# Row maxima of half the score units added on VectorE instead of by a matmul, with all orders drawn anew

## The reference, cut to what matters

```python
h = layernorm(x) * g1 + b1
x = attention(h, h) + x             # 16 heads of 64, 1024 keys: "self"
h = layernorm(x) * g2 + b2
x = attention(h, context) + x       # 16 heads of 64, 154 keys: "cross"
h = layernorm(x) * g3 + b3
p = h @ w1 + b; a, gate = halves of p   # 2 x 1024 columns
x = (a * gelu(gate)) @ w2 + b2 + x
# attention: softmax(q k^T / 8) v for each head, then @ wo + bo
```

## Time and profile before

| | |
|---|---|
| median of 3 runs | 1222.76 us (1222.62 to 1223.83) |
| profiled execution | 1222.66 us, span 1220.6 us |
| TensorE busy | 1186.3 us, 97% of the span |
| VectorE | 767.2 us, 63% |
| ScalarE | 642.3 us, 53% |
| GpSimd | 743.0 us, 61% |
| granted TensorE clock, mean | 0.997 |

### The profile page before, as it was taken

One profiled execution on the slowest core, in us unless ns is written; L12 is line 12 of the kernel. 1 busy time (PEld: TensorE's weight loads), 2 busy tenths in 40 slices (PEclk: granted clock), 3 DMA queues, 4 the chain that ended last, 5 costly groups with the idle time before them and its releaser, 6 DMA issues.

```text
span 1220.6 us, 23620 instructions
## 1 busy us (share of the span) xinstructions
PE 1186.3 (97%) x9385; PEld 776.6 (64%) x9385; DVE 767.2 (63%) x1289; ACT 642.3 (53%) x954; POOL 743.0 (61%) x381
## 2 busy tenths in 40 slices
PE   3899999999999999999999999999999999999998
PEld 3655665566566656666655664666666666678887
DVE  4757566575575576675665756458777877674433
ACT  3447554445445446744544454557855586536432
POOL 1196787886876976877877768864556346321000
PEclk9899999999999999999999999999999999999999
DMA  3010000000000000000000000011111110010000
GB/s 111 14 27 10 6 17 16 5 11 23 6 10 23 6 10 23 6 10 14 14 11 12 10 13 6 23 31 50 48 40 32 33 33 14 15 36 18 18 18 18
DMA packets 63539, 25.76 MB, mean 21 GB/s; under 512 B 34551, under 2 KB 61383, under 8 KB 63431
## 3 DMA queue, kind: packets, MB, share of 16 engines
q1 hardware_dynamic: 63375, 24.25, 7.6%
q10 hardware_dynamic: 56, 0.01, 0.0%
HBM read 21.62 MB, written 2.10 MB: 19 GB/s over the span
## 4 chain that ended last, share of the span: by engine, by line
PE 89%; POOL 4%; ACT 2%; DVE 2%; issue 1%; DMA 1%; SPq 0%; DVEq 0%; POOLq 0%; ACTq 0%
PE psum L858 22%; PE psum L844 22%; PE psum L736 15%; PE psum L721 9%; PE psum L881 7%; PE psum L821 6%; POOL acc L1402 4%; PE psum L941 4%; PE psum L869 3%; PE psum L826 2%; PE psum L895 1%; ACT probs L1273 1%; DVE xr L1084 1%; DMA probs<-in_ctx 1%; DVE m_part L1047 1%
## 5 line engine op out<-in xcount | busy, mean ns | idle before, releaser
L1402 POOL TENSOR_TENSOR acc<-acc,probs 128x1024 f32<-128x1024 f32 x192 | 458.7, 2389 | 70.1 <-ACT probs L1273 49.7
L1273 ACT ACTIVATE probs<-psum 128x1024 f32<-128x1024 f32 (+1 forms) x320 | 317.1, 1031 | 275.6 <-PE psum L844 271.1
L1047 DVE TENSOR_REDUCE m_part<-psum 128x2 f32<-128x1024 f32 x256 | 308.9, 1222 | 223.0 <-PE psum L821 223.0
L858 PE MATMUL psum<-probs,val 128*64 128x512 f32 x1024 | 244.9, 603 | 0.0
L1402 POOL TENSOR_TENSOR acc<-probs 128x1024 f32<-128x1024 f32 (+1 forms) x64 | 152.8, 2388 | 142.2 <-ACT probs L1273 120.3
L1084 DVE SCALAR_TENSOR_TENSOR xr<-psum,d_cols,xr 128x256 f32<-128x256 f32 x512 | 207.8, 476 | 35.1 <-PE psum L881 34.6
L858 PEld LDWEIGHTS psum<-probs,val 128*64 128x64 f32 x1024 | 63.3, 136 | 113.7 <-issue 98.8
L844 PE MATMUL psum<-row_max,minus 64*128 64x512 f32 (+1 forms) x640 | 125.9, 389 | 0.0
L844 PE MATMUL psum<-q_hi,k_hi 64*128 64x512 f32 x512 | 101.6, 393 | 0.3 <-DVE m_part L1047 0.3
L844 PE MATMUL psum<-q_lo,k_hi 64*128 64x512 f32 x512 | 100.8, 389 | 0.0
L844 PE MATMUL psum<-q_hi,k_lo 64*128 64x512 f32 x512 | 100.8, 389 | 0.0
(11 more groups left out here) (147 smaller groups left out, 2132.1 us busy)
## 6 DMA issues: line engine op xcount, KB each, us to landing
xr<-in_x SPq DMA_DIRECT2D x8, 256.0 KB, 5.8
wv_raw<-in_L_xattn_sa_wv SPq DMA_DIRECT2D x8, 256.0 KB, 2.9
wqk_raw<-in_L_xattn_sa_wq SPq DMA_DIRECT2D x16, 128.0 KB, 2.5
wqk_raw<-in_L_xattn_sa_wk SPq DMA_DIRECT2D x16, 128.0 KB, 2.3
wo_raw<-in_L_xattn_sa_wo SPq DMA_DIRECT2D x16, 128.0 KB, 2.4
d_cols<-d_rows SPq DMA_DIRECT2D x128, 2.0 KB, 2.1
wqk_raw<-in_L_xattn_ca_wq SPq DMA_DIRECT2D x16, 128.0 KB, 2.6
probs<-in_L_xattn_ff_w SPq DMA_DIRECT2D x8, 256.0 KB, 3.4
```

What stands on the lines that cost most here:

```text
L858: mm = pe.matmul(psum[d, PVB + half, :], values(J)[0:plan.ks, kt, own], probs[buffer_of(J, u)][0:plan.ks, h, :], start=(kt == 0), stop=(kt ...
L1047: dve.tensor_reduce(m_part[:, half, :, t, kh], psum[:, bank0:bank0 + 2, :], AX.X, ALU.max).then_inc(s_x_read, 1)
L1273: act.activation(probs[buffer_of(J, u)][0:plan.ks, :, :], psum[0:plan.ks, bank0:bank0 + 2, :], ACT.Exp, scale=SCALE).then_inc(s_exp, 1)
L1402: pool.tensor_tensor(total, last if kt == 1 else total, now, ALU.add).then_inc(s_acc, 1)
```

## The change

Units 1, 3, 5, ... 15 of each self pair (`TAKEN_BY_VECTOR`) lose the fourth step. VectorE instead adds a block `less_max` (minus the maxima, spread over all 128 partitions) to the scores while it moves them from PSUM to `probs`; this is the new item U, function `take`. ScalarE then takes their exponential in place. The PSUM buffer of such a unit is given back by U. The even units keep the fourth step, now with `one_row` (ones in rows 0 and 64) and the same `less_max` block.

The maxima of a half, now negated in the reduction, go by one DMA into a scratch tensor in DRAM (M), and from there by one DMA to all 128 partitions (N). N waits for M to land and for all users of the old block. The cross pairs keep their way and use the `less_max` blocks as their buffer; their M waits for that. All written orders are new.

```diff
+TAKEN_BY_VECTOR = (1, 3, 5, 7, 9, 11, 13, 15)
+def on_vector(J, u):
+    return J < NSELF and u in TAKEN_BY_VECTOR
+def taken(J, u):
+    return min(J, NSELF) * len(TAKEN_BY_VECTOR) + sum(v < u for v in TAKEN_BY_VECTOR if J < NSELF)
...
-MOVED = before(lambda p: 16 * 2)
+MOVED = before(lambda p: 16 if p.own else 32)
...
 SELF_ORDER = {
+    "sp": "G@-197.68 W@-114.85 M0@-11.44 N0@-10.62 M1@14.11 N1@27.09 O@38.83 T@53.64",
+    "pe": "P12-@-5.74 K0+@-3.73 S0@-3.58 K1+@-2.78 P13-@-1.64 P14-@-1.42 P15-@-0.29 D-@0.24 S1@3.54 Q0+@4.03 S2@4.11 Q1+@6.99 S3@7.94 Y0.0-@8.14 P0@8.41 P1@8.74 S4@10.18 X0+@10.20 S5@10.42 Y0.1-@10.69 S6@11.02 X1+@12.19 P2@12.57 S7@12.72 Y1.0-@12.98 Y1.1-@15.66 X2+@16.27 P3@16.82 P4@17.25 P5@17.65 X3+@19.47 S8@20.20 X4+@21.02 P6@21.03 S9@21.84 S10@22.09 S11@22.49 X5+@23.04 P7@23.63 P8@23.64 X6+@25.24 X7+@28.87 V0++@30.48 X8+@32.24 V1++@33.23 S12@33.68 S13@34.94 S14@36.14 X9+@36.81 P9@38.15 P10@39.08 P11@39.13 X10+@40.69 S15@41.30 X11+@45.63 X12+@47.02 X13+@47.46 X14+@47.67 X15+@50.32",
+    "dve": "K0+@2.17 K1+@2.88 L1-@7.22 U1@7.73 B-@8.41 U3@9.16 Q0+@9.53 Q1+@11.36 Y0.0-@13.06 X0+@13.32 U5@14.63 Y0.1-@14.99 X1+@15.49 U7@16.29 Y1.0-@17.34 Y1.1-@19.07 X2+@22.43 X3+@29.20 X4+@29.36 U9@29.96 U11@30.37 X5+@30.70 X6+@30.75 X7+@32.90 C0+@34.86 X8+@35.42 U13@37.07 X9+@37.17 X10+@40.85 U15@42.12 X11+@42.16 L0@48.43 X12+@50.77 X13+@56.12 X14+@56.78 X15+@57.47 C1+@58.36",
...
 def release_of(item):
     if kind == "S":
-        return "S", U0[J] + a + 1
+        return ("U", taken(J, a) + 1) if on_vector(J, a) else ("S", U0[J] + a + 1)
...
-        top = [sb(f"row_max{b}", [P, SEQ], F32R) for b in range(2)]
-        minus = sb("minus", [P, P], F32R)
+        less_max = [sb(f"less_max{a}", [P, 2, HALF], F32R) for a in range(2)]
+        one_row = sb("one_row", [P, P], F32R)
...
+        max_rows = nc.dram_tensor("less_max_rows", (2, 2, HALF), F32, kind="Internal").ap()
...
             def move_m(J, a):
...
+                if own:
+                    sp.dma_start(max_rows[a].rearrange("h (p t) -> p h t", p=P),
+                                 m_cols[a][:].bitcast(F32).rearrange("p (h t) -> p h t", h=2)).then_inc(s_m[a], 16)
+                    return
...
+            def spread_m(J, a):
+                sp.wait_ge(s_m[a], MOVED[J + 1])
+                if J:
+                    sp.wait_ge(s_s, U0[J - 1] + 8 * (a + 1))
+                    sp.wait_ge(s_taken, taken(J - 1, 8 * (a + 1)))
+                sp.dma_start(less_max[a][:].bitcast(F32), max_rows[a].partition_broadcast(P)).then_inc(s_less_max[a], 16)
...
             def S(J, u):
...
+                last = 2 if on_vector(J, u) else 3
+                for i, (w, x) in enumerate(((k_hi, q_hi), (k_hi, q_lo), (k_lo, q_hi))):
                     for h in range(2):
+                        mm = pe.matmul(psum[0:plan.ks, bank_of(("S", J, u), h), :], w[rows_of(h), ks], x[rows_of(h), qs], start=(i == 0), stop=(i == last))
+                if last == 3:
+                    for h in range(2):
+                        x = less_max[half][rows_of(h), h, :] if plan is SELF else top[J % 2][rows_of(h), qs]
+                        mm = pe.matmul(psum[0:plan.ks, bank_of(("S", J, u), h), :], one_row[rows_of(h), 0:plan.ks], x, start=False, stop=True)
...
+            def take(J, u):
+                half = u // SELF.kt
+                bank0 = bank_of(("S", J, u))
+                back = user_before(J, u)
+                dve.wait_ge(s_less_max[half], 16 * (J + 1))
+                if back:
+                    dve.wait_ge(s_pv, U0[back[0]] + back[1] + 1)
+                    dve.wait_ge(s_acc, added(*back))
...
+                dve.wait_ge(s_s, U0[J] + u + 1)
+                dve.tensor_tensor(probs[buffer_of(J, u)][:], psum[:, bank0:bank0 + 2, :], less_max[half][:].bitcast(F32), ALU.add).then_inc(s_taken, 1)
...
             def S(J, u):
...
+                if on_vector(J, u):
+                    act.wait_ge(s_taken, taken(J, u) + 1)
+                    act.activation(p, p, ACT.Exp, scale=SCALE).then_inc(s_exp, 1)
+                    return
```

More of the change, by code:

```diff
@@ L161 @@
     "sp": "",
[L162 to L165, removed]
+    "pe": "t0.0@13.94 t0.1@15.70 t1.0@28.06 t1.1@35.50",
+    "dve": "n0@-14.00 n1@-10.99 z0@-7.55 z1@-0.19 l0.0@18.73 l0.1@21.95 l1.0@31.17 l1.1@39.39",
+    "act": "s0@-6.00 y0@-0.00 a0.0@15.35 a0.1@17.36 y1@19.46 a1.0@25.62 a1.1@39.37",
+    "pool": "b0@12.93 b1@62.78",
 }
@@ L473, in block_kernel @@
         w2_lo = [w2_lo_both[:, 4 * i:4 * i + 4, :].rearrange("p f c -> p (f c)") for i in range(2)]
+        top = [t[:].rearrange("p h n -> p (h n)") for t in less_max]
+        max_rows = nc.dram_tensor("less_max_rows", (2, 2, HALF), F32, kind="Internal").ap()
         z_early = acc[1][:].rearrange("p h n -> p (h n)").rearrange("p (t d) -> p t d", t=4)
@@ L483, in block_kernel @@
         s_fill = sem("buffers_filled")
-        s_minus_zero = sem("minus_zeroed")
+        s_row_zero = sem("one_row_zeroed")
         s_vec = sem("vectors_loaded")
@@ L523, in block_kernel @@
         s_m = [sem(f"m_moved{a}") for a in range(2)]
+        s_less_max = [sem(f"less_max{a}_ready") for a in range(2)]
+        s_taken = sem("max_taken")
         s_s = sem("s_ready")
@@ L646, in move_m @@
                     sp.wait_ge(s_x_read, X0[J + 1])
-                if J < 2:
-                    sp.wait_ge(s_fill, FILLS)
-                if J >= 2:
-                    sp.wait_ge(s_s, U0[J - 1])
-                n = 4 if own else 8
-                for h in range(2):
-                    row, q0 = h * DH, a * HALF
-                    cols = m_cols[a] if own else c_cols[J % 2]
-                    sp.dma_start(top[J % 2][row:row + 1, q0:q0 + n * P].bitcast(F32).rearrange("o (p t) -> o p t", p=P),
-                                 cols[:, n * h:n * (h + 1)].bitcast(F32)).then_inc(s_m[a], 16)
+                if own:
+                    after(sp, s_less_max[a], 16 * J)
+                else:
+                    sp.wait_ge(s_s, U0[J if J == NSELF else J - 1])
+                    sp.wait_ge(s_taken, taken(J, 0))
+                if own:
+                    sp.dma_start(max_rows[a].rearrange("h (p t) -> p h t", p=P),
+                                 m_cols[a][:].bitcast(F32).rearrange("p (h t) -> p h t", h=2)).then_inc(s_m[a], 16)
+                    return
+                for h in range(2):
+                    sp.dma_start(top[J % 2][h * DH:h * DH + 1, :].bitcast(F32).rearrange("o (p t) -> o p t", p=P),
+                                 c_cols[J % 2][:, 8 * h:8 * (h + 1)].bitcast(F32)).then_inc(s_m[a], 16)
+            def spread_m(J, a):
[4 more added lines that the diff above has]
+                sp.dma_start(less_max[a][:].bitcast(F32), max_rows[a].partition_broadcast(P)).then_inc(s_less_max[a], 16)
             def move_d(J):
@@ L699, in _ @@
                     move_m(J, a)
+                elif kind == "N":
+                    spread_m(J, a)
                 elif kind == "T":
@@ L838, in S @@
                     pe.wait_ge(s_kq_lo, KQ0[J] + plan.khalf + half + 1)
-                    pe.wait_ge(s_m[half if plan is SELF else 0], MOVED[J + 1])
+                    if plan is CROSS:
+                        pe.wait_ge(s_m[0], MOVED[J + 1])
+                if plan is SELF and not on_vector(J, u):
+                    pe.wait_ge(s_less_max[half], 16 * (J + 1))
                 ks = slice(kt * plan.ks, (kt + 1) * plan.ks)
                 qs = slice(half * HALF, (half + 1) * HALF)
-                for i, (w, x) in enumerate(((k_hi, q_hi), (k_hi, q_lo), (k_lo, q_hi), (minus, top[J % 2]))):
+                last = 2 if on_vector(J, u) else 3
+                for i, (w, x) in enumerate(((k_hi, q_hi), (k_hi, q_lo), (k_lo, q_hi))):
                     for h in range(2):
-                        mm = pe.matmul(psum[0:plan.ks, bank_of(("S", J, u), h), :], w[rows_of(h), ks if i < 3 else slice(0, plan.ks)], x[rows_of(h), qs], start=(i == 0), stop=(i == 3))
+                        mm = pe.matmul(psum[0:plan.ks, bank_of(("S", J, u), h), :], w[rows_of(h), ks], x[rows_of(h), qs], start=(i == 0), stop=(i == last))
[3 more added lines that the diff above has]
+                        mm = pe.matmul(psum[0:plan.ks, bank_of(("S", J, u), h), :], one_row[rows_of(h), 0:plan.ks], x, start=False, stop=True)
                 mm.then_inc(s_s, 1)
@@ L1058, in C @@
                 dve.tensor_reduce(m_cols[a][:, 0:8], m_part[:, a, :, :, :].rearrange("p h t k -> p (h t) k"),
-                                  AX.X, ALU.max).then_inc(s_m_cols, 1)
+                                  AX.X, ALU.max, negate=True).then_inc(s_m_cols, 1)
+            def take(J, u):
[6 more added lines that the diff above has]
+                    dve.wait_ge(s_acc, added(*back))
+                if J == 0 and u == 7:
+                    dve.wait_ge(s_c_hi, KC)
+                dve.wait_ge(s_s, U0[J] + u + 1)
```

(13 more changed lines are left out.)

48 lines of the change are left out of this document (15 added, 33 removed), and 47 rows, old and new, of tables (CROSS_ORDER, OPENING, SELF_ORDER, TURN).

## The result

The changed kernel takes 1220.94 us (median of 8 runs, 1218.54 to 1222.10); the kernel before, in turn with it, 1223.03 us (8 runs, 1222.43 to 1223.83). The ratio is 0.998, with an interval from 0.9971 to 0.9989. The change gains 2.1 us where I had forecast 20.6, and the time lies just outside both ranges that I gave (1193 to 1212, and 1189 to 1220 with the side cases). The profiled execution is the quickest of the eight: 1218.54 us around a span of 1216.6.

The account below looks back on a forecast made before the run. TensorE, busy 97% of the span, was taken as the bound. From 1222.7 us, -29.7 + 1.0 + 5.6 + 1.9 + 4.0 - 2.0 + 1.0 - 2.4 = -20.6 gave 1202; range 1193 to 1212, 1189 to 1220 with side cases.

Parts of the forecast that it names:

- Eight of 16 units lose the fourth step. 8 x 0.232 = 1.86 us a pair.: Self pairs, TensorE: 128 maximum steps removed, on the path, 29.7 us gained in all.
- A self pair's own work becomes 47.07 - 1.86 + 0.35 = 45.56 us.: Self pair, TensorE: work rebuilt from issue spacing, less eight steps, plus one more run of probability-times-value products.
- The walk gives small stalls at S5, X2 and S11, 0.3 to 0.4 us in all.: Self pair: TensorE waits for banks from VectorE at two score units and a row maximum; priced +5.6 us in all.
- Three runs more: +1.0: Whole kernel, TensorE order: eight product runs a self pair instead of seven, one a cross pair instead of two; +1.0 us.
- Opening, -3.4 in all: Opening: earlier context load -2, later first maxima +1, GpSimd's bias addition moved behind its additions -2.4 us.
- TensorE's 1.86 us are not gained: Pair 14: the denominator product stays behind GpSimd's additions, so the removed steps gain nothing there; +1.9 us.
- Normalisation +4: Pairs preparing the second batch and next layer: VectorE's low parts fall into its gapless stretch; +4 us, from 0 to 10.
- The route costs nothing: Maxima through DRAM to all partitions: 7.2 us, with 10.1 us available in the first half, so no cost.
- (a): Self pair, VectorE's gapless stretch: VectorE becomes the bound, 1236 at 2.5 us stall; chance 0.10, partial form 0.10.
- (b): Start of each first half: the maxima's route is late, 1220 if the spread takes 8 us; chance 0.06.
- (c): Self pairs: TensorE's sum comes through whole without stalls, 45.6 us a pair and 1192 in all; chance 0.14.
- ScalarE has over 20 us idle a pair ... nothing: Self pair, ScalarE: odd units' exponentials wait 1.2 us longer for the addition and read SBUF, at no cost.

Follow-up runs that it names:

- e2: Changed kernel with all 16 fourth steps kept and no additions, new orders and route kept, two exponentials moved forward: 47.66 us a plain pair, median 1248.00 us.
- e1: Changed kernel with the odd units' additions left out too, maxima not subtracted there, two exponentials moved forward (measurement only): 46.01 us a plain pair, median 1223.41 us.
- e11: Changed kernel with the orders of the kernel before, all 16 fourth steps, no additions, only the maxima's new route: 47.05 us a plain pair, median 1228.46 us.
- e3: Changed kernel with each addition covering one head of two from pair 1 on (measurement only): 46.02 us a plain pair, median 1212.07 us.
- e12: Changed kernel with the orders of the kernel before and only four additions, units 8, 10, 11 and 14: 47.3 to 47.9 us a plain pair, median 1242.17 us.
- e7: Changed kernel with ten additions, units 12 and 14 besides the eight odd ones: 46.47 us a plain pair, median 1228.44 us.
- e10: Changed kernel with the orders of the kernel before and seven additions, units 1, 9 and 11 to 15: 48.60 us a plain pair, median 1259.16 us.

## Why the prediction was wrong

The direction and the place were right, the size was not: -20.6 forecast, -2.1 in the medians, -4.0 in the profiled spans. Three things carry the miss: the self pair's TensorE sum took no account of waits that the new orders have (0.26 and 0.21 us a pair), the stalls at VectorE were priced 0.24 us a pair too low, and 8.0 us were booked as gains in the cross pairs and the opening where 0.5 were lost. Step by step, each in the prediction's words:

- **"Eight of 16 units lose the fourth step. 8 x 0.232 = 1.86 us a pair."** Failed in size: 1.65 by e2 against e1. I took the spacing of steps for the worth of one. Of the other 0.21, 0.07 are the longer wait ahead of Y0.1 (0.19 in e1, 0.12 in e2). The rest was not taken apart.
- **"A self pair's own work becomes 47.07 - 1.86 + 0.35 = 45.56 us."** Failed. The run more is in it, but the new orders cost 0.61, 0.26 more than that run (e2); 0.12 of it is the wait ahead of Y0.1, the rest was not placed. I counted units and runs and did not ask whether the new sequence keeps TensorE free of waits as the old one did: I had shown "nothing is a stall" for the old order alone.
- **"The walk gives small stalls at S5, X2 and S11, 0.3 to 0.4 us in all."** The stretch was right, and S5 in it; the chain also has S7, which I had not named. Both hang on VectorE. The size was too small: 0.59 by e1 against the change. The three gaps, 0.21 + 0.26 + 0.24, make the 0.7 us between 45.9 and 46.60.
- **"Three runs more: +1.0"** was the balance of 16 more in the self pairs and 13 fewer in the cross pairs, worth -4.6 us there. The cross pairs measured +0.6. Before, one X stood ahead of D and paid the exit of the run of products, 0.38. Now D is ahead of all of them and no X pays for that exit, but a later one starts late (0.45 instead of 0.18) because ScalarE's exponential has not yet given its bank back. Chains of a cross pair, before and after:

```profile
909.78 0.38 PE psum L826 x4
910.16 0.99 PE psum L869 x8
911.16 0.38 PE psum L826 x4
...
912.47 0.18 PE psum L826 x4
```
```profile
904.78 1.00 PE psum L876 x8
905.78 0.38 PE psum L825 x4
...
907.09 0.18 PE psum L825 x4
...
908.21 0.45 PE psum L825 x4
```

  The exit of a run partly covered a wait, and was no price by itself. That this is the mechanism rests on these chains alone; no run took the cross order by itself.
- **Opening, -3.4 in all: measured -0.1.** Its first part held: TensorE starts at 8.25 instead of 10.57, the first projection at 20.74 instead of 24.05. Then the chain goes through VectorE in pair 0:

```profile
20.74 7.90 PE psum L735 x48
...
52.91 1.23 DVE probs L1079
54.14 1.21 DVE k_lo L1046 x2
...
64.13 1.22 DVE probs L1079
...
66.34 1.02 ACT probs L1300
...
67.40 0.49 PE psum L820 x2
```

  In pair 0 VectorE has the additions beside the reductions of two pairs, and TensorE stands behind its work for 2.5, 2.5 and 4.4 us (up to 55.39, 61.52 and 67.40; in the last, two exponentials stand behind VectorE's part). Before, it waited for GpSimd's additions at D instead; the gain of 3.3 us and the 2.4 us of the moved bias addition are both spent on the new waits. I had priced what goes and not what is late next.
- **Pair 14, "TensorE's 1.86 us are not gained"**: right in effect (+0.66 instead of a gain), wrong in cause. The chain of the changed kernel has no GpSimd in pair 14; it does in pair 15, which gained 1.95 us where a plain pair gained 0.46; I had not forecast this pair apart.
- **Normalisation +4**: pairs 1 and 9 are 0.95 and 0.69 us behind what a plain pair gained; 1.6 in these two, within the bounds that I gave.
- **The route costs nothing**: right in the steady pairs (e11: 47.05). The Trainium skill (DMA: Bandwidth & Descriptors, Specifications and "Why small descriptors are slow (HBM only)") says that transfers under 512 bytes are read, modified and written, and I had taken that as a doubled time, an estimate of mine. The trace shows no doubling: 4 KB in pieces of 16 bytes landed in 2.4 us, against 2.0 for the 2 KB moves of the earlier trace rows.
- **Rivals.** (a) is right in its mechanism, in the partial form to which I gave 0.10: a stall of 0.8 to 1.5 us a pair. By the prediction's own count the pair holds 46.60 - 45.56 = 1.04 us beyond TensorE's work, but only 0.59 of it is VectorE's additions (e1), and the rest was there before any addition. Its 1209 to 1220 us were missed because of the cross pairs and the opening. The sign that I gave, over 1 us of waiting for VectorE a pair, did not come. (b) did not occur behind the opening. (c), 45.6 us a pair, was not reached even with no addition at all (46.01).
- **"ScalarE has over 20 us idle a pair ... nothing"** holds by the new orders only (46.02 with the hop in e3, 46.01 without in e1). With the old ones five additions make the pair 1.76 us longer although five steps are gone, and its chain leads to the exponentials of units 15 and 0 that stand behind each other in ScalarE's queue.

## What to carry to other kernels

When work is moved from the bounding engine to one that is 63% busy, do not take the receiving engine's idle time for free: here five additions (35 of 47 us, 75%) cost nothing, and each further one 0.14 to 0.22 us of a step worth 0.206. Runs with few and with all of the units show where that begins; whether it goes by load or by place was not settled. Redrawn orders are a change of their own with a price of their own; a run with the new orders and the old work shows it. And a step's spacing is its price only where nothing beside it waits.

## What the runs showed of the hardware

- 512 KB spread to 128 partitions landed in 3.6 us, a transfer of 4 KB in pieces of 16 bytes to DRAM in 2.4, and the DMA engines went from 0.05 to 0.12 of their time; in the opening of e11 the same two took 1.54 to 3.16 and 3.72 to 4.37.
- The granted clock fell in the last cross pair in some executions. Stretches of e12:

```profile
1080.00:1089.00 9.00, 7.28 (x86) 5.43 (x84) 3.62 (x9) 4.40 (x5) 4.76 (x2) 1.00 0.28 77
1089.00:1098.00 9.00, 9.00 (x25) 2.15 (x26) 5.01 (x12) 2.81 (x5) 3.08 (x2) 0.51 0.00 0
```

  0.51 is the 1.2 GHz level. The product with the values there, 16 matmuls from 1088.96, took 6.85 us instead of 3.58, and the pair 17.42 instead of 12.26. Ahead of the fall TensorE had waited 1.7 us for VectorE's Y (1086.28 to 1087.98). e7 and e10 show the same (17.23 and 17.98): the price is about 5 us in the pair, and the part behind it is another 1.2 to 2.4 us longer. The runs of e7 lie near 1222.5 or between 1226 and 1231.3, which fits; only one of them has a trace. The kernel before had 1.00 there in its profile. No run shows that the wait is the cause.
- The clock of the opening differs between executions: 0.83 or 0.74 between 25 and 45 us, 1.00 or 0.97 from 45 to 100, and D of pair 0 comes between 98.0 and 101.9 in kernels with the same opening. How much of this is the clock is not shown, since these kernels differ in the additions of pair 0 too. A gain of 2 us in a steady part is therefore read from starts, not from one total.
